# A fused wavelet and expert kernel: its wavelet stage written out in a new order per engine

## The reference

```
ll, lh, hl, hh = haar_dwt(norm(x))            # four half-resolution bands of each 2 x 2 cell
bands = concat(ll * exp(s_ll), lh * exp(s_lh), hl * exp(s_hl), hh * exp(s_hh))
low   = einsum('bchw,oc->bohw', bands, w1) + b1     # 256 -> 64 channels
rest  = einsum('bchw,oc->bohw', low, w2) + b2       # 64 -> 256 channels
x1    = x + haar_idwt(split(rest, 4))
```

## Time and profile before

| | |
|---|---|
| median of 3 runs | 2513.83 us (2513.47 to 2518.53) |
| the profiled execution's own time | 2511.39 us |
| its span, first to last instruction | 2509.6 us |
| PE busy | 2124.1 us (85%) |
| DVE busy | 1560.4 us (62%) |
| ACT busy | 1063.9 us (42%) |
| POOL busy | 658.4 us (26%) |
| load of x, 128 KB, issue to landing | 2.9 us (median) |

### The profile page before, as it was taken

One profiled execution on the slowest core, in us unless ns is written; L12 is line 12 of the kernel. 1 busy time (PEld: TensorE's weight loads), 2 busy tenths in 40 slices (PEclk: granted clock), 3 DMA queues, 4 the chain that ended last, 5 costly groups with the idle time before them and its releaser, 6 DMA issues. The chain is left out here.

```text
span 2509.6 us, 38741 instructions
## 1 busy us (share of the span) xinstructions
PE 2124.1 (85%) x12605; PEld 1554.4 (62%) x12605; DVE 1560.4 (62%) x3011; ACT 1063.9 (42%) x2868; POOL 658.4 (26%) x694
## 2 busy tenths in 40 slices
PE   5999991679999987877878878778888699999999
PEld 2555550647777766777767777777777455555554
DVE  4777777645555544444444444444444599999998
ACT  3666663033333322333334444444444545454542
POOL 4777761112222210000000000000000566555662
PEclk9999995589999998999999999999999799999999
DMA  6544440022222210000000000000000355555543
GB/s 135 158 143 143 150 129 22 5 93 85 85 85 85 85 44 0 0 0 0 0 3 0 0 0 0 0 0 0 0 0 0 95 133 130 128 132 132 129 120 80
DMA packets 176399, 158.81 MB, mean 63 GB/s; under 512 B 25976, under 2 KB 126360, under 8 KB 176280
## 3 DMA queue, kind: packets, MB, share of 16 engines
q1 hardware_dynamic: 175768, 156.91, 22.6%
q0 software_dynamic: 512, 0.53, 0.1%
HBM read 56.72 MB, written 67.11 MB: 49 GB/s over the span
## 5 line engine op out<-in xcount | busy, mean ns | idle before, releaser
L1066 PE MATMUL s_ps<-g_yh,g_Tlo 128*128 128x256 f32 x1905 | 336.7, 308 | 211.4 <-DVE g_yh L1094 195.5
L1066 PEld LDWEIGHTS s_ps<-g_yh,g_Tlo 128*128 128x128 f32 x1905 | 257.1, 191 | 289.7 <-DVE g_yh L1094 273.2
L1432 POOL TENSOR_TENSOR g_X<-tm_x,g_X 128x512 f32<-128x512 f32 x64 | 83.3, 1320 | 1052.8 <-DVE tm_m L1512 1052.8
L1140 ACT ACTIVATE g_X<-s_xs 128x256 f32<-128x256 f32 x254 | 177.5, 699 | 382.3 <-DVE g_yl L1084 382.3
L1094 DVE SCALAR_TENSOR_TENSOR g_yh<-s_ps,s_xs 128x256 fp32r<-128x256 f32 x254 | 108.0, 425 | 353.9 <-PE s_ps L1070 353.9
L1521 DVE TENSOR_TENSOR tm_Z<-tm_pg,tm_nd 128x1024 f32<-128x1024 f32 x256 | 299.2, 1211 | 10.4 <-PE tm_pg L1315 10.2
L1070 PE MATMUL s_ps<-g_yl,g_Thi 128*128 128x256 f32 x1905 | 293.3, 284 | 0.0
L1066 PE MATMUL s_ps<-g_yh,g_Thi 128*128 128x256 f32 x1905 | 292.8, 284 | 0.0
L1070 PEld LDWEIGHTS s_ps<-g_yl,g_Thi 128*128 128x128 f32 x1905 | 258.7, 191 | 0.0
L1066 PEld LDWEIGHTS s_ps<-g_yh,g_Thi 128*128 128x128 f32 x1905 | 255.6, 189 | 0.0
L1327 PE MATMUL tm_po<-tm_Z,g_wexp 128*64 128x512 f32 x1024 | 247.7, 605 | 0.0
(11 more groups left out here) (287 smaller groups left out, 4049.5 us busy)
## 6 DMA issues: line engine op xcount, KB each, us to landing
tm_nd<-tm_nS SPq DMA_DIRECT2D x256, 128.0 KB, 2.4
g_X<-in_x SPq DMA_DIRECT2D x128, 128.0 KB, 2.9
x1s<-g_X SPq DMA_DIRECT2D x64, 256.0 KB, 2.4
x1tok<-g_X SPq DMA_DIRECT2D x64, 256.0 KB, 2.7
tm_x<-x2s SPq DMA_DIRECT2D x64, 256.0 KB, 2.9
y<-tm_yo SPq DMA_DIRECT2D x128, 128.0 KB, 2.5
g_X<-x1s SPq DMA_DIRECT2D x32, 256.0 KB, 2.8
x2s<-g_X SPq DMA_DIRECT2D x32, 256.0 KB, 2.0
```

The source lines that it names most:

```text
L1066: pe.matmul(out, t[:, d * P:d * P + P], g.yh[:, :, d:d + 64], start=(t is g.Tlo[i] and d == 0), stop=False)
L1140: act.activation(line(*place(n)), xs[n % RING][:], ACT.Copy).then_inc(stored, 1)
```

## The change

The stage's loop is written out for all 64 chunks, and every engine gets a new order within a step, through small functions (`centre`, `variance`, `low`, ...) called in that order. Where a function is called with c - 3, it works on the chunk three behind.

- The low band: its two products, one for even and one for odd columns, no longer accumulate on partitions 0 to 63 of bank `vl`. Each writes its own half of the partitions of bank `tv`, which the token variance also uses. `lowS` is 128 partitions high, ACT copies all of it, and `Brec` has its rows twice, so that the restoring product adds the two halves.
- The output bias is no longer a row of that product. It is a column per half (`g.b2c`), added by DVE.
- `add_restored`: DVE no longer adds once and then rounds x1 to x1h from SBUF. It forms the sum twice from bank `rec`, first into `x1h` (rounded on writing), then into x in place, each as two SCALAR_TENSOR_TENSOR of 256 columns. It waits until the token centring before it has read `x1h`.
- The chunk buffers are 10 instead of 8, x is loaded 3 chunks ahead instead of 2, the expert weights are loaded in steps 8 to 15 instead of 0 to 7.
- Four semaphores are borrowed from a later stage and cleared in the expert choice by SP.

```diff
-        bcomb = m.sb("bcomb", [P, 2, C + 1])
+        bcomb = m.sb("bcomb", [P, 2, 2, C])
...
-                for low in g.lowS:
-                    dve.memset(low[C:C + 1], 1.0)
+                dve.memset(g.b1[C:P], 0.0)
...
-                dve.tensor_scalar(bcomb[:], tmp[:, 2:4], 0.5, None, ALU.mult).then_inc(rec_ready, 1)
+                dve.tensor_scalar(g.b2c[:], tmp[:, 2:4, C], 0.5, None, ALU.mult)
+                dve.tensor_scalar(bcomb[:], bcast(tmp[:, 2:4, 0:C], 2, 2), 0.5, None, ALU.mult).then_inc(rec_ready, 1)
...
-    AHEAD = 2
+    AHEAD = 3
...
+        xh, xl = ([m.sb(n, [P, N], F32R)] * 2 for n in ("xh", "xl"))
+        x1h, x1l = m.sb("x1h", [P, N], F32R), m.sb("x1l", [P, N], F32R)
...
+                def load(c):
+                    wait(sp, x1_out[c % XBUFS], c // XBUFS * 16)
+                    wait(sp, s["tturned"], c - XBUFS + 1)
+                    wait(sp, s["x1parts"], c - XBUFS + 1)
+                    wait(sp, s["logits"], (c - XBUFS) // 2 * 2 + 2)
                     for t in range(2):
-                        sp.dma_start(xr[u][t * C:t * C + C].rearrange("p (j w) -> p j w", j=JR),
-                                     x_src[u % B, t][:, bass.ds(rows, JR), :]).then_inc(xin[u], 16)
+                        sp.dma_start(buf(c)[t * C:t * C + C].rearrange("p (j w) -> p j w", j=JR),
+                                     x_src[c % B, t][:, c // B * JR:c // B * JR + JR, :]).then_inc(xin[c % XBUFS], 16)
...
+                    if now(c + AHEAD):
+                        load(c + AHEAD)
+                    if 8 <= c < 16:
+                        load_experts(c - 8)
+                    if now(c - 3):
+                        store_x1(c - 3)
+                    if now(c - 4):
+                        store_tokens(c - 4)
...
+                def centre(c):
+                    wait(pe, s["xparts"], c + 1)
+                    wait(pe, s["normed"], c - 1)
+                    pe.matmul(xc[c % 2][:], Cmr[:], xh[c % 2][:], start=True, stop=False)
+                    pe.matmul(xc[c % 2][:], Cmr[:], xl[c % 2][:], start=False, stop=True).then_inc(s["centred"], 1)
+                def variance(c):
+                    wait(pe, s["parts"], c + 1)
+                    wait(pe, s["lnv"], c)
+                    pe.matmul(va[:], Jr[:], sq_hi[:], start=True, stop=False)
+                    pe.matmul(va[:], Jr[:], sq_lo[:], start=False, stop=True).then_inc(s["var"], 1)
+                def low(c):
+                    wait(pe, s["normed"], c + 1)
+                    wait(pe, s["low_s"], c)
+                    wait(pe, s["tln"], (c - 3) // 2)
+                    nv = nn[c % 2].rearrange("p (q v) -> p v q", v=2)
+                    for v in range(2):
+                        last = pe.matmul(tv[v * C:v * C + C, 0:N // 2], g.Alow[:, v], nv[:, v], start=True, stop=True)
+                    last.then_inc(s["low"], 1)
+                def gate_logits(pair):
+                    wait(pe, s["x1"], 2 * pair + 2)
+                    wait(pe, s["glog"], pair)
+                    for half in range(2):
+                        last = pe.matmul(lg[half * C:half * C + C, :], g.Gc, buf(2 * pair + half), start=True, stop=True)
+                    last.then_inc(s["logits"], 2)
+                def token_variance(pair, c):
+                    wait(pe, s["tsquared"], 2 * pair + 2)
+                    wait(pe, s["low_s"], min(c + 1, CHUNKS))
+                    for half in range(2):
+                        last = pe.matmul(tv[half * C:half * C + C, :], g.J[:, C - E0:C + E0], tsq[half],
+                                         start=True, stop=True)
+                    last.then_inc(s["tvar"], 2)
+                def token_centre(c):
+                    wait(pe, s["x1parts"], c + 1)
+                    wait(pe, s["tsquared"], c)
+                    pe.matmul(tc[:], Cmr[:], x1h[:], start=True, stop=False)
+                    pe.matmul(tc[:], Cmr[:], x1l[:], start=False, stop=True).then_inc(s["tcentred"], 1)
+                def turn(c):
+                    wait(pe, s["x1"], c + 1)
+                    wait(pe, s["tcopied"], c)
+                    for j in range(JR):
+                        last = pe.transpose(tt[:, j * P:j * P + P], buf(c)[:, j * W:j * W + W], g.ident)
+                    last.then_inc(s["tturned"], 1)
+                def restore(c):
+                    wait(pe, s["low_s"], c + 1)
+                    wait(pe, s["x1"], c)
+                    for v in range(2):
+                        last = pe.matmul(rec[:, v * (N // 2):(v + 1) * (N // 2)], g.Brec[:, v], lowS[c % 2],
+                                         start=True, stop=True)
+                    last.then_inc(s["rec"], 1)
+                for c in steps:
+                    if now(c):
+                        centre(c)
+                    if now(c - 1):
+                        variance(c - 1)
+                    if now(c - 4):
+                        token_centre(c - 4)
+                    if now(c - 2):
+                        low(c - 2)
+                    if now(c - 5) and c % 2 == 0:
+                        gate_logits((c - 5) // 2)
+                        token_variance((c - 5) // 2, c - 2)
+                    if now(c - 3):
+                        turn(c - 3)
+                    if now(c - 2):
+                        restore(c - 2)
...
+                def copy_low(c):
+                    wait(act, s["low"], c + 1)
+                    wait(act, s["rec"], c - 1)
+                    act.activation(lowS[c % 2], tv[:, 0:N // 2], ACT.Identity, bias=g.b1[:]).then_inc(s["low_s"], 1)
...
+                def low_of_square(c):
+                    wait(pool, s["high"], c + 1)
+                    pool.tensor_tensor(sq_lo[:], sq[c % 2], sq_hi[:].bitcast(F32), ALU.subtract).then_inc(s["parts"], 1)
+                def low_of_x(c):
+                    wait(pool, s["xhigh"], c + 1)
+                    wait(pool, s["centred"], c)
+                    pool.tensor_tensor(xl[c % 2][:], buf(c), xh[c % 2][:].bitcast(F32), ALU.subtract
+                                       ).then_inc(s["xparts"], 1)
+                def low_of_x1(c):
+                    wait(pool, s["x1"], c + 1)
+                    wait(pool, s["x1high"], c + 1)
+                    pool.tensor_tensor(x1l[:], buf(c), x1h[:].bitcast(F32), ALU.subtract).then_inc(s["x1parts"], 1)
+                low_of_x(0)
+                for c in steps:
+                    if now(c - 3):
+                        low_of_x1(c - 3)
+                    if now(c):
+                        low_of_square(c)
+                    if now(c + 1):
+                        low_of_x(c + 1)
...
+                def add_restored(c):
+                    wait(dve, s["rec"], c + 1)
+                    xv = buf(c).rearrange("p (q v) -> p v q", v=2)
+                    hv = x1h[:].rearrange("p (q v) -> p v q", v=2)
+                    wait(dve, s["tcentred"], c)
+                    for v in range(2):
+                        last = dve.scalar_tensor_tensor(hv[:, v], rec[:, v * (N // 2):(v + 1) * (N // 2)],
+                                                        g.b2c[:, v:v + 1], xv[:, v], ALU.add, ALU.add)
+                    last.then_inc(s["x1high"], 1)
+                    for v in range(2):
+                        last = dve.scalar_tensor_tensor(xv[:, v], rec[:, v * (N // 2):(v + 1) * (N // 2)],
+                                                        g.b2c[:, v:v + 1], xv[:, v], ALU.add, ALU.add)
...
+                high_of_x(0)
+                for c in range(CHUNKS + LAG + 2):
+                    if now(c - 3):
+                        add_restored(c - 3)
+                    if now(c):
+                        high_of_square(c)
+                    if now(c + 1):
+                        high_of_x(c + 1)
+                    if now(c - 6) and c % 2 == 1:
+                        scale_logits((c - 6) // 2)
+                    if now(c - 1):
+                        normalise(c - 1)
+                    if now(c - 3):
+                        copy_tokens(c - 3)
...
+                for sem in g.scan_sems[1][2:6]:
+                    sp.sem_clear(sem)
...
-        g.xr = [v.take(N) for _ in range(8)]
+        g.xr = [v.take(N) for _ in range(XBUFS)]
```

More of the change, by code:

```diff
@@ L308, in wavelet_mixer, with now, buf @@
         tok_dst = g.x1tok.rearrange("b j w x -> b w j x")
+        steps = range(CHUNKS + LAG)
+        def now(c):
+            return 0 <= c < CHUNKS
+        def buf(c):
+            return xr[c % XBUFS]
         with nc.Block() as block:
@@ L330, in load_experts @@
                             "e p o -> p e o")).then_inc(g.experts_loaded, 16)
[L332 to L343, removed]
-                    if valid(k4, u4, U, CHUNKS):
-                        wait(sp, s["tcopied"], k4 * U + u4 + 1)
-                        rows = k4 * (JR * U // B) + (u4 // B) * JR
-                        sp.dma_start(tok_dst[u4 % B][:, bass.ds(rows, JR), :],
```

(40 more changed lines are left out.)

240 lines of the change are left out of this document (55 added, 185 removed).

## The result

| | before | after |
|---|---|---|
| median | 2513.65 us (2510.52 to 2518.53, 4 runs) | 2676.42 us (2658.75 to 2683.59, 4 runs) |
| span of the profiled execution | 2509.6 us | 2674.7 us |
| mean from centring to centring, chunks 4 to 63 | 5.403 us | 7.973 us |
| PE, DVE, ACT, POOL busy over the span | 85, 62, 42, 26% | 80, 60, 39, 25% |

The changed kernel is slower: the ratio of its time to that of the kernel before is 1.0635, with a 95% interval of 1.0581 to 1.069. The forecast was 2664 us, range 2620 to 2732.

What follows compares the result with a forecast made beforehand. PE was taken as nearly full before; afterwards a PE-DVE-POOL ring bounds the wavelet stage: 7.41 us, 7.6 with the port, 7.95 with the clock. 59 x (7.95 - 5.40) = +150 gives a median of 2664 us, range 2620 to 2732.

Steps and rivals of the forecast that it cites:

- the three places: Wavelet stage: add_restored waits for token_centre behind centre, low_of_x1 for add_restored, the next centre for low_of_x behind low_of_x1.
- the ring: Wavelet stage: PE, DVE and POOL work in series from one centring to the next, 7.41 us against 5.40.
- A: Rival: the ring doesn't close, about 4.7 us a chunk in the wavelet stage, -41 us, 2473; chance 5%.
- D: Rival: DVE's added passes eat what PE saves, 5.4 us a chunk, 2514; chance 1%.
- The stage's sum: Wavelet stage: 59 steps, each going from 5.40 to 7.95 us, +150 us in all.
- head, tail: Wavelet stage before chunk 4 and its drain after the last centring: 0 each, the head with 3 us either way.
- the quick step: Wavelet stage: one turn of the ring at the full clock, port included, 7.6 us.
- three subtractions, with the port: POOL's three subtractions back to back in the ring, 3.84 us, plus 0.2 for meeting DVE's casts.
- clock, in the mean of a step: PE at both clock levels in turn, the low one a quarter of the time: 0.25 x 1.4, mean step 7.95 us.
- the upper end: DVE's cast of x(c+1) waits out low_of_x1 and low_of_square at the port: +0.36 us a step.
- Rival B: Clock low almost throughout the wavelet stage, 9.0 us a chunk, +212 us, 2726; chance 22%.
- Rival C: The ring stands, clock holds at 1.00, casts slip in: 7.45 us a chunk, +121 us, 2635; chance 23%.

Runs made afterwards that it cites:

- e8: Kernel before, with x1h and x1 each formed from the bank by two passes, no bias column, old order kept: 2515.78 us, ratio 0.9997.
- e9: Kernel before, with the low band on column tiles, bias as a column, sum formed once in two passes: 2498.57 us, ratio 0.9928.
- p1: Changed kernel, with x rounded by ScalarE instead of DVE: 2654.46 us, ratio 1.0557.
- e5: Changed kernel, with six products that nobody reads filling PE's idle time at each step's end: 2651.58 us, ratio 1.0534.
- e4: Changed kernel, with the low band's two products issued twice: 2664.69 us, ratio 1.058.
- e3: Changed kernel, with x1 formed once and x1h made by a cast behind the wait, orders kept: 2596.08 us, ratio 1.0315.
- e7: e1 with five products that nobody reads at the end of PE's odd steps: 2532.15 us, ratio 1.0074.
- e1: Changed kernel, with PE's token centring moved first in the step, ahead of centre(c): 2560.91 us, ratio 1.0174.
- g1: e1 with x rounded on ScalarE and POOL's order x1, x, square: 2511.59 us, ratio 0.9984.
- g2: g1 with the logits moved from PE's even steps into the odd ones: 2510.11 us, ratio 0.9971.

## Why the prediction was right

The mechanism stood: the three places that were named close the ring, and rivals A and D are out. The stage's sum was 59 x 2.55 = 150 and is 151.6; the 12 us by which the median lies over the forecast are about what head, tail and the part behind the stage add. The ring's terms, from the quick step above:

| term | predicted | measured |
|---|---|---|
| PE, centre to the end of token centring | 1.93 | 512.20 + 0.39 - 510.91 = 1.68 |
| PE to DVE | 0.06 | 0.10 |
| four passes of the sum | 1.44 | 513.48 + 0.87 - 512.69 = 1.66 |
| DVE to POOL | 0.08 | 0.08 |
| three subtractions, with the port | 3.84 + 0.2 | 517.19 + 1.26 - 514.43 = 4.02 |
| POOL to PE | 0.06 | 0.05 |
| the quick step | 7.6 | 7.59 |
| clock, in the mean of a step | 0.35 | 0.37 |

- The 7.6 came out on two errors that cancel. PE's term was 0.25 too long: behind the first pair (0.34 apart) the four single-pass products that follow start 0.24 apart, where I had read 0.67 and 0.54 from pair to pair in the earlier trace rows. The passes were 0.22 too short. The rows that I took the earlier trace rows have no column among their operands. The first of the two passes in e8's groups by line:

```profile
L515 DVE SCALAR_TENSOR_TENSOR wm_x1h<-wm_rec,g_X 128x256 fp32r<-128x256 f32 x128 | 48.1, 417 | 45.3 <-PE wm_tc L395 45.3
```

and in those of the kernel after:

```profile
L534 DVE SCALAR_TENSOR_TENSOR wm_x1h<-wm_rec,g_b2c,g_X 128x256 fp32r<-128x256 f32 x128 | 56.2, 481 | 189.3 <-PE wm_tc L411 188.4 <-PE wm_rec L424 0.9
```

- With the bias as a column a pass takes 481 ns, with an immediate 417: 0.06 more each, 0.25 in the ring. e8 has the same stage and the same operands otherwise, but the old order; that the order is not the reason is shown by e9, with a column in the old order (groups by line):

```profile
L511 DVE SCALAR_TENSOR_TENSOR g_X<-wm_rec,g_b2c,g_X 128x256 f32<-128x256 f32 x128 | 55.5, 476 | 0.8 <-PE wm_rec L370 0.8
```

- The port: 0.18 to the second subtraction, as p1 shows by taking it away, against the 0.2 chosen, and 0.1 to the first. The cast of x waits out x1's subtraction (514.43 to 515.81), runs, and ends at 516.10; the square's, started at 515.77, ends late. It got in after the first of the two, so the upper end, after the second, did not come. The Trainium skill, SBUF — State Buffer, "SBUF: two separate sides", gives the lock; that a cast which waited through one subtraction gets in ahead of the next one is what these rows add.
- The clock was right in size and kind: both levels in turn, 22 us in all (e5). That the cost came out at 0.37 for 0.35 is luck in part, since the quarter of the time was a judgement with no row behind it. 13 of 60 steps begin low, and the 16 that fall later add the rest; the mean clock of 0.84 puts a third of the time at the low level. The slow step is not what was described either: 12 of the 13 hold the logits, for which the prediction had a full PE and 9.3. Most take 8.85, since PE is back at the high level by the logits (257.53, 1.02) and waits 1.5 to 2.2 for POOL at the end. So the low level lengthens the ring by PE's term, 2.93 for 1.68, and never fills PE.
- Rival B is out: PE at the low level came back from it. The kernel that the prediction takes from the Trainium skill, TensorE: Matmul & The Clock Gate, "HAM oscillation — how this bites in real kernels", waited longer between its bursts than PE does here (2.57 us at most), so it does not speak for B. Rival C would have had 1.00, which of the kernels with the whole ring only e5 has, by its added products.
- PE was to be busy about 60% and is busy 313.27 of 450 us, 70%, since its products take longer at the low level: two quick steps in a row (chunks 15 and 16) hold 5.90 us of idle time in 15.14, which is 61% busy.
- Low on column tiles takes 513.02 - 512.51 = 0.51, predicted 0.47. That the saving is slack in the ring is shown by e4, which takes PE's time back at no price; e9 shows it worth 16 us where there is no slack.
- Head and tail were put at 0 and are +2.1 and +0.6.
- Not foreseen: the 10.7 us behind the stage. They don't follow the change. From the last centring to the end of the span it takes 2144.8 us before and 2156.2 after, but 2142.4 in e3, which has the ring and its low clock, and 2156.8 in e8, whose stage runs as before's; all the profiled runs lie between 2142.0 (e7) and 2157.1 (e4). The windows show a lower clock there at starts of scans in the profiled run of the kernel after. What decides it from run to run stays open.

What the runs corrected is my picture of the way out. In e1 I counted on the chain of centring, square, cast and two subtractions at the full clock, in g1 and g2 on PE's load, and overlooked the waits for POOL and for the shared bank; each came to light only when the one above it was gone.

## What to carry to other kernels

Where each engine's order is written out by hand, walk from one item of the repeat to its next through every queue on the way. A wait on a single buffer that stands at the head of one engine's step, for an item behind the first of another's, puts these engines in series, though none is full; four passes over the sum cost 67 to 80 us in such a ring and nothing (0.9997) outside it. Price each part of a change in the order that it will run in, and after opening a ring look for the next chain before counting PE's load as the bound.

## What the runs showed of the hardware

- A SCALAR_TENSOR_TENSOR of 128x256 from a bank takes 481 ns with a column as its scalar (kernel after; 476 in e9) and 417 with an immediate (e8).
- A DVE cast that waits through one GpSimd subtraction gets in ahead of the next: of two subtractions back to back the second took 1441 ns, and 1263 with the cast on ScalarE (p1).
- With PE idle 0.6 to 2.6 us at the end of each step, 13 of 60 steps began at the low clock and 16 more fell to it early, not all and not none. Work in PE's slack that nobody reads made the kernel quicker, by 22 us in the stage of e5, where the granted clock was 1.00.
- Single-pass products of 512 columns start 0.34 us apart in the first pair of the quick step (510.91 and 511.25), and 0.24 apart in the run behind it (511.25 to 512.20). The kernel before has 0.33 for a pair without idle time ahead of it (358.06 and 358.39), so the wait is not the reason, and what is wasn't tested.
